# The output projection moved from a stage of its own into the attention loop, one batch behind it

## The reference, cut to what matters

```python
mod = silu(c) @ wmod                       # per batch: sa, ca, ga, sb, cb, gb
h = layernorm(x) * (1 + ca) + sa
q, k, v = heads(ln(h) @ Wq + bq), ...      # rope on q and k
probs = softmax(causal(q @ k.T / 4))
att = (probs @ v)                          # 16 heads side by side: [B, L, 256]
x = x + ga * (h + att @ Wo + bo)           # the output projection and the gated residual
h = layernorm(x) * (1 + cb) + sb
x = x + gb * experts(h)                    # 8 experts on gathered token rows (of the first two batches)
```

## Time and profile before

| | us |
|---|---|
| median of 3 runs (lowest to highest) | 3257.47 (3256.44 to 3257.87) |
| the profiled execution | 3256.85 |
| its span, from first to last instruction | 3255.1 |
| busy over the span: PE / DVE / ACT / POOL | 2952.9 / 2328.9 / 1713.4 / 1019.2 |
| mean granted TensorE clock, share of full speed | 0.952 |

### The profile page before, as it was taken

How to read it: one execution, slowest core, us unless ns; L and a number is a source line. 1 busy time by engine, 2 the same in 40 slices (tenths; PEclk the granted TensorE clock), 3 DMA queues, 4 the chain that set the end, 5 groups by cost and what they waited for, 6 DMA issues and landing times. The chain is left out here.

```text
span 3255.1 us, 50330 instructions
## 1 busy us (share of the span) xinstructions
PE 2952.9 (91%) x18199; PEld 1403.3 (43%) x18199; DVE 2328.9 (72%) x3444; ACT 1713.4 (53%) x3591; POOL 1019.2 (31%) x1366
## 2 busy tenths in 40 slices
PE   2888998885999999999999999999999979975997
PEld 0444444441444444444444444444444347753664
DVE  5999999995777777777777777777777425543221
ACT  1444444430677777777777777777777731111111
POOL 3888888862122111112221111112221100003232
PEclk7999999996999999999999999999999989987999
DMA  2466666657244444444444444444444246663332
GB/s 77 138 180 191 191 191 191 184 156 175 55 95 93 95 100 100 100 96 92 94 95 92 97 100 100 100 96 90 95 92 92 48 173 259 259 230 110 78 100 56
DMA packets 175373, 403.11 MB, mean 124 GB/s; under 512 B 34556, under 2 KB 87202, under 8 KB 158518
## 3 DMA queue, kind: packets, MB, share of 16 engines
q1 hardware_dynamic: 168984, 391.37, 47.1%
q0 software_dynamic: 6144, 8.52, 1.5%
HBM read 240.65 MB, written 161.31 MB: 123 GB/s over the span
## 5 line engine op out<-in xcount | busy, mean ns | idle before, releaser
L946 DVE TENSOR_REDUCE mx<-ps 128x2 f32<-128x1024 f32 (+3 forms) x1216 | 1371.2, 1166 | 396.6 <-PE ps L1034 301.3
L992 ACT ACTIVATE prob<-ps 128x512 f32<-128x512 f32 (+1 forms) x2560 | 1251.4, 561 | 539.0 <-PE ps L1052 530.0
L1027 PE MATMUL ps<-k_rows,q_rows 96*128 96x512 bf16 (+3 forms) x3072 | 909.9, 332 | 40.6 <-DMA k_rows<-k_parts 33.1
L1052 PE MATMUL ps<-q_rows,k_rows 99*128 99x512 bf16 (+3 forms) x3072 | 908.5, 329 | 14.5 <-ACT prob L992 6.0
L885 POOL TENSOR_SCALAR_AFFINE_SELECT prob<-prob 128x512 f32<-128x512 f32 x512 | 318.6, 634 | 1453.8 <-ACT prob L992 1453.8
L1071 PE MATMUL ps<-prob,v_rows 128*32 128x512 f32 (+3 forms) x6144 | 628.6, 497 | 0.0
L1052 PEld LDWEIGHTS ps<-q_rows,k_rows 99*128 99x128 bf16 x3072 | 273.3, 98 | 598.8 <-ACT prob L992 359.8
L688 PE MATMUL ps<-w_all,x_t 128*128 128x512 f32 (+1 forms) x1024 | 427.9, 543 | 0.0
L1027 PEld LDWEIGHTS ps<-k_rows,q_rows 96*128 96x128 bf16 x3072 | 290.4, 98 | 269.8 <-DVE mx L946 60.4
L1034 PE MATMUL ps<-mask_b,unit_b 128*128 128x128 bf16 (+2 forms) x1408 | 348.5, 248 | 0.0
L1071 PEld LDWEIGHTS ps<-prob,v_rows 128*32 128x32 f32 x6144 | 134.7, 108 | 245.7 <-ACT prob L992 122.8
(11 more groups left out here) (143 smaller groups left out, 2707.4 us busy)
## 6 DMA issues: line engine op xcount, KB each, us to landing
k_rows<-k_parts SPq DMA_DIRECT2D x384, 128.0 KB, 7.5
v_ones<-v_st SPq DMA_DIRECT2D x64, 512.0 KB, 9.0
v_rows<-v_ones SPq DMA_DIRECT2D x64, 512.0 KB, 9.5
att<-o_sb SPq DMA_DIRECT2D x128, 256.0 KB, 3.2
att_b<-att SPq DMA_DIRECT2D x16, 2048.0 KB, 10.9
q_parts<-stage SPq DMA_DIRECT2D x192, 128.0 KB, 2.4
k_parts<-stage SPq DMA_DIRECT2D x192, 128.0 KB, 2.4
q_rows<-q_parts SPq DMA_DIRECT2D x64, 384.0 KB, 4.6
```

The costliest lines, as they stand in the source:

```text
L946: dve.tensor_reduce(dst, src, AX.X, ALU.max).then_inc(a_free, 1)
L992: nc.scalar.activation(prob[:, (g * NPC + i) % RING, h, 0:w], src, ACT.Exp).then_inc(exp_done, 1)
L1027: ins = pe.matmul(ps[:, at, col:col + w], q[0:ROWS, g, h, i * P:(i + 1) * P], k[0:ROWS, g, h, k0:k0 + w], start=(r == 0), stop=True, skip_ ...
L1052: ins = pe.matmul(ps[:, PS_B + bank(g, n), at:at + w], k[0:AUG, g, h, j * P:(j + 1) * P], q[0:AUG, g, h, q0:q0 + w], start=True, stop=True)
```

## The change

phase3 is gone. Its work becomes 64 jobs of two token tiles each (job j: batch j // 4, quarter j % 4), and step u of phase2 does job u - 6. The path of the data changes as well: SP fetches the numerators of a finished batch from DRAM as rows, already transposed (`num`, 16 heads by 16 rows, two transfers of 8 heads), and its 16 x 1024 denominators as a [128, 128] tile (`den`); DVE inverts that tile in one instruction (`invert`); SP saves the reciprocals to DRAM and reads them back with each head's row repeated for 16 partitions (`spread_reciprocals`, two transfers of 8 heads); POOL multiplies numerators and reciprocals in four instructions on 128 x 512 elements (`normalise`); PE then needs no transposes. A job's matmuls stand in slot 4, whose second bank was unused; DVE adds the residual there with one instruction per job (`add_rows`), and the next fill into these banks waits for it. In SP's list the second-half store and `maxima` now come ahead of the loads of unit u + 3, and at g = 0 a `fetch`, at g = 1 the save and spread of reciprocals come ahead of them too. Six jobs are left for the end of phase2, four of them after the last batch's numerators have gone through DRAM.

```diff
+        BEHIND = 6
+        def job_of(u):
+            return u - BEHIND if u >= BEHIND else None
 # SyncE
+            def fetch(b):
+                p, half = b % 2, b // 2
+                for c in range(2):
+                    sp.wait_ge(o_stored[c], (b + 1) * NG * DMA)
+                rows = att_d[b].rearrange("g (h n) t -> (g h) n t", h=HG)
+                reuse(sp, rec_done, b)
+                sp.dma_start(den[:, :], rows[:, DH, :].rearrange("h (x t) -> h x t", t=P)).then_inc(den_in, DMA)
+                reuse(sp, out_done, (b - 1) * PAIRS)
+                for k in range(KC):
+                    sp.dma_start(num[:, p, k, :], rows[8 * k:8 * k + 8, 0:DH, :]).then_inc(num_in[p], DMA)
+                sp.dma_start(gate[:, p], mods_d[b, M_GA, :].partition_broadcast(P)).then_inc(small_in[p], DMA)
+                sp.dma_start(ob[:, p], out_bias_d[b]).then_inc(small_in[p], DMA)
+                reuse(sp, x2_stored[p], half * DMA)
+                sp.dma_start(res[:, p], resid_d[b]).then_inc(res_in[p], DMA)
+            def save_reciprocals(b):
+                sp.wait_ge(rec_done, b + 1)
+                sp.dma_start(rec_d[b % 2].rearrange("h (x t) -> (h x) t", t=P), rec[:, :]).then_inc(rec_saved, DMA)
+            def spread_reciprocals(b):
+                sp.wait_ge(rec_saved, b * DMA + DMA)
+                reuse(sp, att_ready, b * PAIRS)
+                for k in range(KC):
+                    src = rec_d[b % 2, 8 * k:8 * k + 8, :].rearrange("h (o t) -> h o t", o=1).to_broadcast([8, DH, L])
+                    sp.dma_start(rec_b[:, k, :], src).then_inc(rec_in, DMA)
...
                     was = prior(un)
-                    if not (final and g):
-                        wait_apart(sp, pv_done, was[2] * NPC + NPC)
-                        load(unit(was[0], was[1] + NG))
                     store(was, 1)
+                if g == 1 and b >= 1:
+                    save_reciprocals(b - 1)
                 if not (final and g == NG - 1):
                     maxima(unit(b, g + 1))
+                if g == 0 and b >= 1:
+                    fetch(b - 1)
+                if g == 1 and b >= 1:
+                    spread_reciprocals(b - 1)
+                if u and not (final and g):
+                    sp.wait_ge(pv_done, was[2] * NPC + NPC)
+                    load(unit(was[0], was[1] + NG))
                 store(un, 0)
+                if g == 2 and b >= 2:
+                    store_rows(b - 2)
 # GpSimd: after piece 6 of a step with g == 1
+            def normalise(b):
+                pool.wait_ge(num_in[b % 2], (b // 2 + 1) * KC * DMA)
+                pool.wait_ge(rec_in, (b + 1) * KC * DMA)
+                for r in range(PAIRS):
+                    at = slice(r * 2 * P, (r + 1) * 2 * P)
+                    pool.tensor_tensor(num[:, b % 2, :, at], num[:, b % 2, :, at], rec_b[:, :, at], ALU.mult) \
+                        .then_inc(att_ready, 1)
 # VectorE: invert at slot 5 and gated (wg) at slot 12 of a step with g == 1, add_rows at slot TURN of every step
+                dve.tensor_tensor(rows, ps[:, bank, :].rearrange("p (r n) -> p r n", r=2), rows, ALU.add) \
+                   .then_inc(x2_done, 1)
 # TensorE
                 if s == TURN:
...
+                    if half == 1 and j is not None:
+                        project(j, PS_OUT)
                     return
                 if half == 0 and s - 2 == TURN:
                     reuse(pe, m_left, u)
+                    if j is not None:
+                        pe.wait_ge(x2_done, j + 1)
...
+            def project(j, bank):
+                b, r = j // PAIRS, j % PAIRS
...
+                pe.wait_ge(att_ready, j + 1)
+                for t in (2 * r, 2 * r + 1):
+                    o = ps[:, bank, (t % 2) * D:(t % 2) * D + D]
+                    pe.matmul(o, ones3[:, :], ob[:, b % 2, :], start=(t % 2 == 0), stop=False, skip_group_check=True)
+                    for k in range(KC):
+                        ins = pe.matmul(o, num[:, b % 2, k, t * P:(t + 1) * P], wg[:, b % 2, k, :], start=False,
+                                        stop=(k == KC - 1), skip_group_check=True)
+                ins.then_inc(out_done, 1)
```

More of the change, by code:

```diff
@@ L764, in phase2 @@
     PS_A, PS_B, PS_O = 0, 4, 7
+    PS_OUT = PS_A + 1
+    PS_TAIL = (PS_A + 3, PS_A + 1)
     BANKS = 3
@@ L909, in prologue @@
                 parts(unit(0, 0))
-            steps(pool, prologue, step)
+            steps(pool, prologue, step, lambda: normalise(LAST))
         @block.vector
@@ L946, in largest, with invert, gated, add_rows @@
                 dve.tensor_reduce(dst, src, AX.X, ALU.max).then_inc(a_free, 1)
-            def whole(un, first=False):
-                for s in range(NS):
-                    if s == 2 and not first:
+            def invert(b):
+                dve.wait_ge(den_in, b * DMA + DMA)
+                reuse(dve, rec_saved, b * DMA)
+                dve.reciprocal(rec[:, :], den[:, :]).then_inc(rec_done, 1)
+            def gated(b):
+                dve.wait_ge(small_in[b % 2], (b // 2 + 1) * (2 * DMA))
+                reuse(dve, out_done, (b - 1) * PAIRS)
+                for k in range(KC):
+                    ins = dve.tensor_tensor(wg[:, b % 2, k, :], wo[:, k, :], gate[:, b % 2, :], ALU.mult)
+                ins.then_inc(wg_done, 1)
+            def add_rows(j, bank):
+                b, r = j // PAIRS, j % PAIRS
+                rows = res[:, b % 2, 2 * r:2 * r + 2, :]
+                dve.wait_ge(res_in[b % 2], (b // 2 + 1) * DMA)
+                dve.wait_ge(out_done, j + 1)
+                dve.tensor_tensor(rows, ps[:, bank, :].rearrange("p (r n) -> p r n", r=2), rows, ALU.add) \
+                   .then_inc(x2_done, 1)
+            def whole(un, now=None, first=False):
+                for s in range(NS):
+                    if now is not None and now[1] == 1 and now[0] >= 1 and s == 5:
+                        invert(now[0] - 1)
+                    if now is not None and now[1] == 1 and now[0] >= 1 and s == 12:
+                        gated(now[0] - 1)
+                    if un is not None and s == 2 and not first:
                         finish(prior(un))
-                    if s != TURN:
+                    if un is not None and s != TURN:
                         largest(un, s)
-                    elif not first:
+                    elif un is not None and not first:
                         negate(prior(un))
+                    if s == TURN and now is not None and job_of(now[2]) is not None:
+                        add_rows(job_of(now[2]), PS_OUT)
             def prologue():
@@ L961, in step @@
             def step(un, ahead):
-                if ahead is not None:
-                    whole(ahead)
-                elif un[1] == NG - AHEAD:
+                if ahead is None and un[1] == NG - AHEAD:
                     final = unit(LAST, NG - 1)
@@ L967, in step, with epilogue @@
                     negate(final)
+                whole(ahead, now=un)
+            def epilogue():
+                for j in range(JOBS - BEHIND, JOBS):
+                    if j == LAST * PAIRS:
+                        invert(LAST)
+                        gated(LAST)
+                    add_rows(j, PS_TAIL[j % 2])
             dve.tensor_copy(unit_b[:, :], ident[:, :]).then_inc(consts, 1)
             dve.tensor_copy(mask_b[:, :], mask[:, 384:512]).then_inc(consts, 1)
-            steps(dve, prologue, step)
+            steps(dve, prologue, step, epilogue)
         @block.scalar
@@ L1102, in _ @@
                 weigh(unit(LAST, NG - 1), i)
[L1106 to L1196, removed]
-            def work(b, half, p):
-                for t in range(T):
-                    act.wait_ge(nt_done, b * T + t + 1)
-                    reuse(act, c_done, b * T + t - 1)
-                    nc.scalar.copy(n_t[:, t % 2], ps[:, PS_T + t % 2, 0:D].rearrange("p (k n) -> p k n", k=KC)) \
-                      .then_inc(nt_copied, 1)
-            loop(act, work)
-        @block.tensor
-        def _(pe):
-            def work(b, half, p):
-                pe.wait_ge(att_in[p], half * DMA + DMA)
-                for t in range(T + 2):
-                    s = t % 2
-                    if t < T:
-                        reuse(pe, norm_done, b * T + t - 1)
-                        for g in range(NG):
-                            ins = pe.transpose(ps[:, PS_A + s, g * P:(g + 1) * P], att[:, p, g, t * P:(t + 1) * P],
-                                               ident[:, :])
-                        ins.then_inc(at_done, 1)
-                    if 1 <= t <= T:
-                        r = t - 1
-                        pe.wait_ge(norm_done, b * T + r + 1)
-                        reuse(pe, nt_copied, b * T + r - 1)
-                        for k in range(KC):
-                            ins = pe.transpose(ps[:, PS_T + r % 2, k * P:(k + 1) * P],
-                                               norm[:, r % 2, k * P:(k + 1) * P], ident[:, :])
```

(16 more changed lines are left out.)

49 lines of the change are left out of this document (44 added, 5 removed).

## The result

The change made the kernel slower: 3452.66 us in the median of 4 runs (3441.98 to 3457.11) against 3257.44 us before, a ratio of 1.0596 with a 95% interval of 1.0572 to 1.0619. The forecast was 3152, with 5% for slower. The profiled execution took 3441.98 us; its mean granted clock is 0.913, against 0.952 before.

What follows compares the result with a forecast made beforehand. PE was taken to bound the attention loop, busy 29.94 of 30 us. The sum was 3256.85 - 288.2 (phase3) + 38 (tail) + 126 (PE's jobs) + 4 (DVE) + 15 (SP) = 3152 us; own range 3115 to 3190, 8 in 10 3120 to 3212.

Steps and rivals of the forecast that it cites:

- SP's queue and the loads: Loads behind maxima, fetch and spread: just in time at g = 0, 1 us put per batch, 15 us in all.
- the far bound: At g = 0, fetch at the k rows' 135 GB/s takes 17 us; loads end at +41, 10.6 us late.
- 0.8 us of room: At g = 0, loads forecast to end at +29.8, needed at +30.6, counted from the step's first score matmul.
- half-engine rival: Numerators and spread, eight heads outermost, use half the DMA engines: 39 us more, tail up to 5, 3190 to 3196; 22%.
- slow rival: Fetch and spread move at the k rows' rate, loads come late at g = 0 and 1: 195 us, 3332; 5%.
- nothing is put in: POOL's four products, 5.2 us a batch, delay no masking if reciprocals are back by +23; expected +18 to +21.
- The tail: From the last copy to phase4's first transfer, 38 us come back of phase3's 288.2, bounds 33 and 45.
- The job's 2.2 us: PE's added projection time per job in slot 4: 56 jobs make 123 us, with the last two steps 126.
- the two waits of the earlier trace: PE's short waits in slot 4, 0.22 us for DVE and 0.40 for ACT, of which 0.25 was taken off.
- The start of the maxima at +11.4: SP's maxima follow POOL's parts, put about 2.1 us later than +9.3 because exponentials come after the job.
- the 15 us put for SP's issuing: 1 us in each of 15 batches for what is not smooth in SP's issuing.
- the 4 for DVE: PE waiting for one late maximum, 0.3 us in each of 15 batches: 4 us, between 0 and 22.

Runs made afterwards that it cites:

- e1: Changed kernel with numerators and reciprocals moved with 16 rows of a head outermost instead of 8 heads, same order: 3225.76 us, 0.9896 of the kernel before.
- e6: Changed kernel with only POOL's products moved to the g = 2 step and jobs 7 steps behind: 3446.68 us, 1.0591 of the kernel before.
- e5: Changed kernel with 16 rows outermost, fetch and spread behind the loads, and POOL's products a step later: 3137.32 us, 0.9628 of the kernel before.
- e8: As e5, but the last batch's gate, bias and residual are fetched within the last step: 3132.37 us, 0.9619 of the kernel before.
- e3: Changed kernel with fetch and spread behind the loads, POOL's products at g = 2, jobs 7 steps behind: 3143.10 us, 0.9647 of the kernel before.
- e7: As e1, but gate, bias and residual go behind the loads, numerators stay ahead: 3152.00 us, 0.9672 of the kernel before.

## Why the prediction was wrong

**The step that failed** is in "SP's queue and the loads": "the numerators go to 128 partitions in 4 KB rows as phase3's loads did, so I take the first", the 410 GB/s. Its nearest row shared the size of the rows, but not the outermost dimension, and the price of every other term at g = 0 and 1 hung on it. The keys landed at +40.5 (1681.24) instead of +29.8; the far bound given there was +41. The number of that bound came true, but not by its reason, the k rows' rate for all 2.3 MB: the numerators ran on half of the engines (0.49 and 145 GB/s at 1656 where 410 was put), and the last of the loads as well (0.48 and 96 at 1678). With 0.8 us of room the choice between the bounds was all that stood between no stall and 10 us.

**The half-engine rival (22%)** named the mechanism, and the earlier trace rows against the tail's 0.50 show it. Its size was wrong, 39 us and up to 5 in the tail: e1, which mends the form alone, is 227 us below the changed kernel. It halved the engines and left each at 26 GB/s, where each moves 16; it let the other half go on with the loads, while by e1 6.7 us of the stall at g = 0 came from the form; and it put nothing on g = 1.

**The slow rival (5%)** described the end state, 13 us a batch from "the k rows' rate"; measured are 20, of which PE waits 14.6. What it lacked most is the clock. In the changed kernel waits of 9.6 us in the mean made the steps at g = 0 11.8 longer, in e1 waits of 3.2 made them 5.1 longer: behind the wait the granted clock is 0.50 to 0.51, the lower of its two levels, 1.2 of 2.4 GHz, while PE is already busy. That is some 5 us a batch over two stalls, a quarter of the loss.

**POOL: "nothing is put in".** That stood on reciprocals back at +18 to +21. With the maxima issued at +11.4 that is 7 to 10 us behind them; in the step shown it was 18.5 (1695.51 to 1713.97), and PE waited 6.1 us for the masking. The condition was stated, +23, and it failed with the price of the same transfers. e6 shows that this term alone is worth nothing while the loads are late.

**The tail: 38 forecast, 49.8 measured.** Counted from the last copy, the spread was forecast for +10.6 and came at +18.9, because its forerunner, the save, queued behind numerators on half of the engines and behind the residual; POOL's start was forecast 5.7 us after that and came 10.9 after it. From POOL's start to phase4's first transfer it took 20.1 us, 1.2 less than forecast. With the form mended the tail is 42.1 and 41.9 (e1, e5), with the residual fetched earlier as well 36.9 (e8).

**What was right.** The job's 2.2 us: plain steps are 30.4 us in all eight kernels with the projection in the loop. In the step after those shown above its two tiles start at 1729.70 and 1730.97 and the next work at 1732.14, 2.44 us where the earlier trace rows has 2.45. The step grew by 2.2, as behind the job the two waits of the earlier trace rows are gone. Those two rows are waits of the weight loads (PEld), not of PE as the working has it; the number held all the same:

```profile
1729.70 0.28 PE L1176 MATMUL ps<-ob_b,ones 3*128 3x256 bf16 x1
...
1730.97 0.28 PE L1176 MATMUL ps<-ob_b,ones 3*128 3x256 bf16 x1
1731.18 1.13 PE L1178 MATMUL ps<-wg,num 128*128 128x256 f32 x4
1732.14 0.27 PE L1189 MATMUL ps<-q_rows,k_rows 99*128 99x256 bf16 x1
```

The start of the maxima at +11.4 (measured +11.5) and of the fetch at +13.3 (+13.3) were right, and so were the durations (groups by line, as the earlier trace rows; forecast 1.308 and 0.678):

```profile
L975 POOL TENSOR_TENSOR num<-num,rec_b 128x512 f32<-128x512 f32 x64 | 78.8, 1263 | 292.6 <-DMA rec_b<-rec_den 292.6
```
```profile
L1050 DVE TENSOR_TENSOR res_b<-ps,res_b 128x512 f32<-128x512 f32 x64 | 44.3, 692 | 201.7 <-PE ps L1178 201.7
```

With the stalls gone (e3, e5, e7, e8) the kernel ends between 3132 and 3152 us, at the forecast or up to 20 us below it. The sum was sound but for the transfers, though that e7 meets it is luck: the 15 us put for SP's issuing and the 4 for DVE did not appear (in e3 every step is plain), and the tail was longer than its 38.

**Slips without effect.** DVE's 23 us of work belong to a window of 30 us, not to a step of 28.2; its room is 6 us, not 5. The loads before the change ended 11 to 12 us ahead of need, not 15. The range of 3115 to 3190 is narrower than the sum of the bounds that it names, 3111 to 3209.

**Open.** Why each engine moves 12 to 18 GB/s in the spread and 26 in phase3's loading was not taken apart: e1 shows that it is not the count of engines. e3 moved POOL's products along with the order; the order of both transfers alone was not run. How much of the 5.1 us left in e1 is this rate, and how much the loads' own 135 to 221 GB/s, was not separated either.

## What to carry to other kernels

Before pricing a transfer by a row of the trace, compare the outermost dimension and not only the bytes and the length of the rows; where no row of that form exists, let the slow bound decide whether anything with a due time may stand behind it in the same queue. Put transfers without a due time behind those that have one: here this order, with POOL's products moved to match (e3), turned a loss of 6% into a gain of 3.5%, with the transfers in their slow form. When a wait is taken away and nothing is gained, look for a second wait beside it with the same cause.

## What the runs showed of the hardware

The spread, two transfers of 0.5 MB, ran at a DMA share of 0.49 to 0.51 and 123 to 127 GB/s with 8 as outermost dimension, and at 1.00 to 1.12 and 197 to 295 GB/s with 16 (e1): the form doubled the engines at work and left the rate of each at 12 to 18 GB/s, while a store beside it moved by estimate 26. In e1 a wait of PE of 2.6 us was followed by a stretch at a granted clock of 0.51; the step was 4.3 us longer, so that stretch cost another 1.7.
